# Cross attention, scored by two heads at a time: eight places for other work per batch in place of thirteen

## The reference, cut to what matters

```python
def xattn(tokens, context, Wq, Wk, Wv, Wo, bo):
    Q = _split_heads(tokens @ Wq)          # tokens: layer-normed x, (8, 256, 256)
    K = _split_heads(context @ Wk)         # context: (8, 256, 192)
    V = _split_heads(context @ Wv)
    scores = jnp.einsum('bhnd,bhmd->bhnm', Q, K) * SCALE
    attn = jax.nn.softmax(scores, axis=-1)
    out = jnp.einsum('bhnm,bhmd->bhnd', attn, V)
    out = out.transpose(0, 2, 1, 3).reshape(b, n, h * d)
    return x + out @ Wo + bo
```

## Time and profile before

| what | value |
| --- | --- |
| median of three runs | 2886.88 us |
| profiled execution, device time | 2861.61 us |
| its span | 2859.8 us |
| TensorE busy | 2322.8 us, 81% |
| VectorE busy | 1285.6 us, 45% |
| ScalarE busy | 1063.0 us, 37% |
| GpSimd busy | 605.3 us, 21% |
| TensorE's granted clock, mean | 0.892 |
| batch 0 of the first stage, from its first score on | 88.25 to 111.80 us |
| batch 0 of the second and of the third stage | 1587.51 to 1611.99, 2318.20 to 2341.01 us |

### The profile page before, as it was taken

The page is one execution under the profiler, slowest core; times in us unless marked ns, Lnnn a source line. Parts: engine busy times, 40 slices in busy tenths (PEclk is TensorE's granted clock), DMA queues, the critical chain, the costliest instruction groups (busy, mean ns, idle before and its releaser), DMA issues. The chain is left out here.

```text
span 2859.8 us, 42520 instructions
## 1 busy us (share of the span) xinstructions
PE 2322.8 (81%) x13268; PEld 1681.7 (59%) x13269; DVE 1285.6 (45%) x2878; ACT 1063.0 (37%) x2493; POOL 605.3 (21%) x584
## 2 busy tenths in 40 slices
PE   2897298569798898799796897998999189739998
PEld 1564198334465674366575564557999056518887
DVE  3564300569765417856522564200000356464554
ACT  0464132224455423355521464213444035513332
POOL 0000200217421325711332000310000410023443
PEclk9799599679799899889897899998999589969999
DMA  6650332110000000000003661213220366100001
GB/s 205 118 121 15 132 134 85 32 37 0 23 0 0 34 1 15 16 6 0 12 1 70 116 117 48 74 46 118 93 100 18 97 130 127 28 13 28 22 22 36
DMA packets 115117, 163.73 MB, mean 57 GB/s; under 512 B 14315, under 2 KB 102110, under 8 KB 109886
## 3 DMA queue, kind: packets, MB, share of 16 engines
q1 hardware_dynamic: 109078, 148.68, 20.0%
q0 software_dynamic: 4608, 12.59, 1.3%
q10 hardware_dynamic: 1320, 1.03, 0.2%
HBM read 114.57 MB, written 47.32 MB: 57 GB/s over the span
## 5 line engine op out<-in xcount | busy, mean ns | idle before, releaser
L929 DVE TENSOR_REDUCE xa_mx<-ps 128x2 f32<-128x512 f32 x384 | 255.8, 689 | 201.2 <-PE ps L597 194.1
L787 ACT ACTIVATE xn_tok<-ps 128x512 f32<-128x512 f32 x384 | 227.6, 602 | 174.4 <-PE ps L605 172.8
L1436 PE MATMUL ps<-ex_tiles,ex_w 128*128 x1792 | 212.7, 278 | 7.4 <-issue 3.9
L1436 PEld LDWEIGHTS ps<-ex_tiles,ex_w 128*128 128x128 f32 x1792 | 212.2, 195 | 11.0 <-issue 8.2
L597 PE MATMUL ps<-xa_ks,xa_qs 48*128 48x256 f32 (+1 forms) x768 | 179.5, 343 | 43.5 <-DVE xa_mx L929 18.5
L1442 PE MATMUL ps<-ex_w,ex_h 128*128 128x256 f32 x896 | 202.7, 380 | 0.0
L597 PEld LDWEIGHTS ps<-xa_ks,xa_qs 48*128 48x128 f32 (+1 forms) x768 | 116.1, 203 | 132.4 <-issue 73.2
L1960 PE MATMUL ps<-lo_w,lp_hs 128*128 128x512 f32 x384 | 174.5, 606 | 4.7 <-ACT lp_hs L2004 2.8
L1442 PEld LDWEIGHTS ps<-ex_w,ex_h 128*128 128x128 f32 x896 | 166.3, 191 | 19.9
L605 PE MATMUL ps<-xa_qs,xa_ks 49*128 49x256 f32 (+1 forms) x768 | 171.3, 329 | 0.7 <-ACT xn_tok L787 0.7
L1456 ACT ACTIVATE ex_h<-ps,ex_b 128x128 f32<-128x128 f32 x296 | 108.6, 367 | 152.6 <-PE ps L1436 132.2
(11 more groups left out here) (331 smaller groups left out, 5240.0 us busy)
## 6 DMA issues: line engine op xcount, KB each, us to landing
xa_ks<-x_keys SPq DMA_DIRECT2D x144, 128.0 KB
xa_qs<-x_queries SPq DMA_DIRECT2D x144, 128.0 KB, 4.1
ex_w<-in_L0f_w_dram SPq DMA_DIRECT2D x16, 1024.0 KB, 6.8
...
```

Source lines behind the costliest of these rows:

```text
L787: nc.scalar.activation(pT[:, h % SLOTS].rearrange("p k q -> p (k q)"), c.ps[:, S_BANK + (HEADS * b + n) % 3], ACT.Exp).then_inc(exped.sem, 1)
L929: nc.vector.tensor_reduce(mx[:, half, :, col], c.ps[:, M_BANK + h % 2].rearrange("p (t n) -> p t n", t=2), AX_X, ALU.max).then_inc(max_put ...
L1436: ins = nc.tensor.matmul(c.ps[:, f % 4, 0:P], w1[:, par, k, f * P:(f + 1) * P], tile_of(n)[:, k], start=(k == 0), stop=(k == KD - 1))
```

## The change

In all four loops a step holds two heads: `for k in range(STEPS)` with eight steps, in which heads 2k and 2k + 1 are scored, reduced or exponentiated one right behind the other. The waits of each head are the same. The other work of a batch is dealt to the eight places behind the pairs. The rows of batch b + 3 are turned at the end of batch b (before: those of batch b + 2 at the start of batch b), and those of batch 2 ahead of batch 0.

```diff
-            def step(b, n):
-                if b + 1 < B:
-                    if n == 0:
...
-                for t in range(2):
+            def step(b, k):
+                for n in (2 * k, 2 * k + 1):
                     if b + 1 < B:
-                        score(b + 1, n, t)
+                        if n == 0:
+                            pe.wait_ge(*k_in[(b + 1) % 3](16 * K_LOADS * ((b + 1) // 3 + 1)))
+                            pe.wait_ge(*q_in[(b + 1) % 2](16 * 6 * ((b + 1) // 2 + 1)))
+                        pe.wait_ge(*max_put(HEADS * (b + 1) + n - 1))
                     if b >= 0:
-                        score_T(b, n, n ^ 1, t)
+                        if n % HALF == 0:
+                            pe.wait_ge(*max_in[n // HALF](32 * b + 32))
+                        pe.wait_ge(*exped(HEADS * b + n - 2))
+                    for t in range(2):
+                        if b + 1 < B:
+                            score(b + 1, n, t)
+                        if b >= 0:
+                            score_T(b, n, n ^ 1, t)
...
             for b in range(B):
-                for n in range(HEADS):
-                    step(b, n)
...
+                for k in range(STEPS):
+                    step(b, k)
+                    if k == 0:
                         turn_maxima(b, 1)
+                        if b:
+                            weigh(b - 1, CH - 1)
+                    elif k == 1 and b + 2 < B:
+                        project_queries(b + 2)
+                    elif k == 2:
                         if b:
                             turn_out(b - 1, 0)
                         weigh(b, 0)
+                    elif k == 3:
+                        if b + 3 < B:
+                            project_keys(b + 3)
+                        if b:
+                            turn_out(b - 1, 1)
+                    elif k == 4:
+                        weigh(b, 1)
                         if b + 1 < B:
                             turn_maxima(b + 1, 0)
+                    elif k == 5:
+                        if b + 1 < B:
+                            project_values(b + 1)
+                        if b:
+                            turn_back(b - 1)
+                    elif k == 6 and b:
                         output(b - 1)
+                    elif k == 7:
                         weigh(b, 2)
+                        if b + 3 < B:
+                            turn_rows(b + 3)
```

111 lines of the change are left out of this document (43 added, 68 removed).

## The result

The changed kernel took 2819.05 us (median of four executions, 2811.68 to 2824.49), the kernel before 2885.20 on the same chip (four, 2876.33 to 2888.95). The ratio is 0.976, with a 95% interval of 0.974 to 0.979: 66 us gained where 27 were forecast, and outside the range. In the five rounds of a second session it was 0.978 (0.973 to 0.983).

What follows compares the result with a forecast made beforehand. TensorE's own stream was taken as the bound. Gains of 9.2 us (full batches) and 17.4 (others), 26.6 in all, took the profiled 2861.6 to 2835; carrying over 0.9% gave 2860, 8-in-10 range 2842 to 2887.

Steps and rivals of the forecast that it cites:

- Step 1: Full batches: eight pairs of 0.67 us replace ten singles and three pairs, 0.95 us less, waitless TensorE stream 20.02 us.
- Step 2: Full batches: old TensorE waits of 1.31 us go, new ones behind VectorE sum to 1.19 us, period 21.2 us.
- the walk: The prediction's timing of the new order, place by place through a batch, giving 1.19 us of waits per full batch.
- Step 3: Split query rest and copy add 0.45 us per full batch in the second stage; 0.1 us off in the third.
- Step 4: ScalarE's queue: maxima's way through DRAM takes 6.7 to 7.9 us, slack 8.2; 0.15 us charged per batch for lateness.
- the other batches: Per stage, batch 0 gains 1.4 us, batch 5 1.9, batch 6 1.0, batch 7 1.5; 17.4 us in all.
- rival 3: Gain given back: waits double to 2.5 us per batch and TensorE's clock falls again, about 2882 us; chance 0.12.
- Rows of batch 2 turned ahead of batch 0: 0: Turning the rows of batch 2 ahead of batch 0 was forecast to gain nothing.
- The carried 0.9%: Timed median lies 0.9% above the profiled execution; the same difference carried over takes 2835 us to 2860.
- 1 (DRAM): The maxima's way through DRAM sets the batch; at 10 us a full batch takes 24.8, total 2900 us; chance 0.14.
- 2 (all waits hidden): All waits fall under other work: full batches at 20.1 us, total 2843 us; chance 0.10.
- 4 (pairs do not save): Second head of each pair waits, 0.19 us lost eight times, 2872 us; no own chance, inside the forecast's 0.62.

Runs made afterwards that it cites:

- chunk_between: The kernel before with chunk 2 weighed behind head 14 instead of head 13, its copy behind 15 instead of 14; ratio 0.997, stages 607.4 us.
- copies_and_chunk: The kernel before, batches 5 to 7 alone: two ScalarE copies one head earlier, chunk 2 and its copy behind head 15; ratio 0.992, end 199.7 us.
- pairs_last_batches: The kernel before with heads of batches 5, 6 and 7 in pairs and their other work at its new places; ratio 0.985, end 185.5 us.
- queries_earlier: The kernel before, batch 0 alone: queries of batch 2 projected a head earlier, VectorE's query rest behind maximum 4 instead of 6; ratio 0.998, front 193.5 us.
- rows_as_before: The changed kernel with the rows of batch b+2 turned at the start of batch b, as before; 2835.10 us, ratio 0.982, stages 566.6 us.
- maxima_not_awaited: The changed kernel without TensorE's wait for the row of maxima, that row left out of the transposed scores; ratio 0.978, stages 551.4 us.
- pairs_old_places: The changed kernel with heads still in pairs but the other work at its old places; 2878.01 us, ratio 0.995, stages 615.5 us.
- pairs_first_batches: The kernel before with heads of prologue and batch 0 in pairs, their other work at its new places; ratio 0.998, front 194.5 us.
- before_again: The kernel before, unchanged, profiled a second time; 2873.32 us, stages 617.5 us.

## Why the prediction was wrong

The direction and the bound were right, and so was the mechanism in full batches; the sum was half of what came, since the other batches gained for reasons that it had not priced. By its own steps:

**Step 1, pairs, right.** TensorE in batch 2 of stage 1 after the change, in the manner of the earlier trace rows: pair 0 is followed by the maxima's turn after 0.66, pair 1 by the queries after 0.67.

```profile
131.32 0.38 PE L597 MATMUL ps<-xa_ks,xa_qs 49*128 49x256 f32 x1
...
131.98 0.44 PE L635 MATMUL ps<-eye,xa_mx 128*128 128x128 f32 x2
132.43 1.07 PE L646 MATMUL ps<-xn_tok,xa_v 128*32 128x256 f32 x16
133.43 0.38 PE L597 MATMUL ps<-xa_ks,xa_qs 49*128 49x256 f32 x1
...
134.10 2.00 PE L579 MATMUL ps<-xn_T,xa_wq 128*128 128x256 f32 x8
...
143.40 0.41 PE L635 MATMUL ps<-eye,xa_mx 128*128 128x128 f32 x2 [0.17 <-DVE xa_on L943]
...
151.69 0.66 PE L561 MATMUL ps<-eye,xa_row 128*128 128x128 f32 x4
152.28 0.38 PE L597 MATMUL ps<-xa_ks,xa_qs 49*128 49x256 f32 x1
```

**Step 2, waits, right in place, a little too large.** 20.96 less the waitless 20.02 leaves 0.94 of waits, where the walk had 1.19. By the starts of the matmuls, the turn of the maxima waits 0.17 for the division (walk 0.18), step 5's second head 0.37 (0.36), step 6's projection 0.12 (0.1); step 3 waits 0.17 (0.27), step 5's first head 0.13 (0.28). One reason is the 0.87 that the walk took from the start of a maximum to the scores two heads later: here it is 0.73 (143.17 to 143.90). VectorE stands still before the key rest, with the division and the maxima of step 4 behind it, to the tenth as walked (they start at 143.17, walked 143.2):

```profile
141.88 0.75 DVE L911 SCALAR_TENSOR_TENSOR xa_khl<-ps,xa_anyk,xa_khl 128x512 fp32r<-128x512 f32 x1 [1.42 <-ACT xa_khl L749]
142.54 0.25 DVE L941 RECIPROCAL xa_rec<-ps 128x16 f32<-128x16 f32 x1
142.82 0.42 DVE L943 TENSOR_TENSOR xa_on<-ps,xa_rec 128x256 f32<-128x256 f32 x1
143.17 1.97 DVE L932 TENSOR_REDUCE xa_mx<-ps 128x2 f32<-128x512 f32 x3
```

The old wait of 0.70 at head 0 was most likely VectorE's maximum of head 14, as read: in chunk_between the maximum starts elsewhere and head 0 follows it after the same 0.90. Why that is more than the 0.73 of other heads is not shown.

**Step 3, second and third stage, mis-sized.** Charged 0.45 for the split query rest, measured 0.2 to 0.3 (21.16 to 21.23 against 20.96); the third stage is 0.1 to 0.16 shorter, as written.

**Step 4, the maxima's way through DRAM, right for full batches, its bound wrong.** Charged 0.15 per full batch; TensorE's waits for the maxima at the ends of the twelve full batches come to 1.8 us in one execution and 3.6 in the other, 0.15 and 0.30 each. But the way was bounded by 7.9 us, and behind the change it was longer at the end of batch 0: 8.9 in stage 1 and 9.0 in stage 3 (7.9 and 8.8 in the second execution), where the kernel before took 6.7 and 6.8.

```profile
100.01 0.27 ACTq L777 DMA_DIRECT2D x_maxima<-xa_mxT  x1
108.93 0.35 PE L597 MATMUL ps<-xa_ks,xa_qs 49*128 49x256 f32 x1 [2.31 <-DMA xa_qs<-x_maxima]
...
2294.62 0.27 ACTq L777 DMA_DIRECT2D x_maxima<-xa_mxT  x1
2303.65 0.35 PE L597 MATMUL ps<-xa_ks,xa_qs 48*128 48x256 f32 x1 [2.55 <-DMA xa_qs<-x_maxima]
```

The DMA engines were busy 0.75 and 0.78 of these two batches, 0.58 and 0.64 of the same two before. Denser traffic as the cause fits that, but no run shows it apart from the rest. The 1.7 us of batch 6, which the prediction set beside 6.7 to 7.9, ends at the issue of the reading half and not at the scores; the like figure of the send at 105.08 is 3.9 us (read issued at 109.01).

Steps 2 to 4 together: a full batch without a wait for the maxima gained 1.3, 1.15 and 1.4 us where 0.9, 0.5 and 0.9 were forecast; with those waits in, the middle gained 10.5 for 6.9.

**The step that failed: the other batches, 17.4 forecast.** The front and the end gained 43.8, less some 4 for what of full batches lies in them. (a) *Batches 5 to 7*, 4.4 per stage forecast, some 8 measured in stage 1 (2.45 + 1.67 + 3.77). The walk took ScalarE's exponentials in batch 7 for a load that stays. Before, TensorE waited there for ScalarE's order: 6.8 to 7.6 us per end part for ScalarE, 3.8 to 4.7 for VectorE; after, 2.8 and 2.5 to 2.7. I had the new stream walked, and never the old one: the waits of 0.94, 1.16 and 1.44 stood in the trace before, at one place. Some 12 of the 27.6 us come without pairs; the others are the pairs' own, at least as to VectorE's part, which copies_and_chunk leaves at 4.8 in stage 1 and pairs_last_batches brings to 2.5.

(b) *The front*, 5.9 forecast and 16.2 measured. By its pieces, over the three stages and as means of two executions: the prologue went from 60.3 to 57.3, where nothing was forecast; batch 0 from 71.8 to 67.5, 4.4 less for the forecast's 4.2; batch 1 up to its add from 67.5 to 58.6, 8.8 less where the forecast had a full batch's 1.7. So batch 0 came out in the sum alone, and that was luck: its three stages gained 0.6, 3.0 and -0.8 (1.5, 4.3 and 0.1 in the second executions). In stages 1 and 3 its send came 2.8 and 1.4 us earlier, but the way through DRAM behind it was 2.2 longer in both. The big miss is batch 1. The prediction counted it as a full batch, though it took 25.36 in the earlier trace rows, and 23.80 and 23.70 in the other two stages, against 22.3: the clock is lower behind the wait at its start. After the change it takes 22.38, 21.55 and 22.23. The prediction had that fall of the clock on the table, as a loss in rival 3, and did not count it as a gain when the wait goes. queries_earlier shows the cause for stage 2, where an earlier query rest alone shortens the wait and keeps the clock; over the three stages it brings 6.0 of the 16.2, since stage 1 lost by it.

**"Rows of batch 2 turned ahead of batch 0: 0"** was too little as well: rows_as_before gives 7 to 9 us for the moved rows altogether, 4 of them as waits for the maxima.

**The carried 0.9%** from the profiled execution to the median was the second term that failed: it added 25 us, where the changed kernel's median lies 7 us above its profiled execution (2811.68 to 2819.05) and 20 above in the second session (2808.03 to 2828.32). So of the 41 us between forecast and result 23 stand between the 2835 and the 2811.68 of the profiled execution, and 18 here. The profiled executions differ by 50 us in the first pair and 65 in the second, the timed medians by 66; the stages make 48 and 60 of that. What adds the rest in the timed runs is not shown; the rest of the program, which took 2249 to 2292 us from one execution to another, is room enough.

**The rivals.** 1 (DRAM) fell for the full batches by maxima_not_awaited; at the end of batch 0 the way through DRAM sets the length in stages 1 and 3. 2 (all waits hidden) got nearest in number and was wrong in cause: 0.94 of waits are left. 3 (given back) and 4 (pairs do not save) fell; pairs_old_places shows what 4 would have looked like.

Open: why the moved rows shorten the maxima's way, why it is longer in batch 0 after the change, and some 8 us of the front, which pairs_first_batches and the full batch behind it (5.1 + 2.9) do not explain.

## What to carry to other kernels

Walk the old order with the same care as the new one, batch by batch, the half-empty last ones above all: what a re-deal gains there is the old order's waits, and each stands in the trace with its releaser. Grouping two users of the same banks paid here with 1.4 us or more of other work behind each group of a full batch; with the other work at its old places the grouping alone brought nothing (615.5 us of stages beside 612.6), at the new ones 54. A copy that stands in a queue behind work for a later item makes its reader wait for that item.

## What the runs showed of the chip

- A wait can have a second price: behind 3.43 us idle TensorE's granted clock fell to 0.50 for the next 5 us and 0.85 for the 5 after. Of the eight other profiles with batch 0 head by head and its query rest in its old place seven show 0.50 in that slice of stage 2 and one 0.65. The length of the wait does not tell by itself whether it happens: behind 1.93 us (queries_earlier) and 2.00 us (rows_as_before) the clock stayed at 1.00, behind 1.08 us (before_again) it was 0.50 two us later.
- The same program part ran at a granted clock of 0.85, 0.73 or 0.69 over 100 us in different executions. The whole way between two stages, some 1300 us, took 13 to 21 us more in the two with the lower ones. That is more than most of the edits here.
- The same transfer there and back, from the send of the maxima to the scores that use them, took 6.7 us before and 8.9 after the change in stage 1, with the DMA engines busy 0.58 and 0.75 of the batch.
- A wait that the profile puts down to issue need not be one: the 0.47 us at head 0 in chunk_between ends 0.90 us behind the start of VectorE's maximum of head 14, as the wait of 0.70 at head 0 in the kernel before does.
